# Fused attention and FFN block on one core: moved squares in two halves, the qkv weight split, one LayerNorm and the low parts placed elsewhere

## What is computed

```python
h = _layernorm(x, axis=-1) * (1 + ca) + sa
# _L0_attn_ref: 16 query heads in 4 groups, each group with one key and one value head, D = 128
qkv = jnp.einsum('bsh,ph->bsp', x, weight_qkv).reshape(b, s, NKV, GROUP)
scores = jnp.einsum('bsgqd,btgd->bgqst', q, k) * scale
attn = jax.nn.softmax(jnp.where(causal, scores, jnp.finfo(scores.dtype).min), axis=-1)
out = jnp.einsum('bgqst,btgd->bsgqd', attn, v).reshape(b, s, NH * D)
x = x + ga * jnp.einsum('bse,he->bsh', out, weight_proj)
h = _layernorm(x, axis=-1) * (1 + cb) + sb
x = x + gb * _L0_ffn_ref(h, ...)   # Hadamard transforms, up and gate (1024), silu, down
```

## Time and profile before

| | us |
|---|---|
| median of 3 runs | 1001.2 |
| lowest and highest | 998.78, 1009.32 |
| the profiled execution | 1000.3 |
| its span in the trace | 998.5 |
| turns 0 to 7 in the trace | about 50 to 840 |
| of these turn 3 | about 362 to 464 |
| FFN weights and FFN | about 840 to the end |

### The profile page before, as it was taken

How to read it: one execution, slowest core, us unless ns; L and a number is a source line. 1 busy time by engine, 2 the same in 40 slices (tenths; PEclk the granted TensorE clock), 3 DMA queues, 4 the chain that set the end, 5 groups by cost and what they waited for, 6 DMA issues and landing times.

```text
span 998.5 us, 14544 instructions
## 1 busy us (share of the span) xinstructions
PE 925.7 (93%) x5140; PEld 797.4 (80%) x5140; DVE 641.3 (64%) x1342; ACT 510.5 (51%) x1062; POOL 567.5 (57%) x687
## 2 busy tenths in 40 slices
PE   6979999899889998999899989999999899999998
PEld 5767788878778887888778877787878787888887
DVE  6566658666866576647664767476747666775554
ACT  3456556654556465646564646465646665431111
POOL 1466928792778277837793678458846876120000
PEclk9989999999989998999999989999999999999999
DMA  6033203320322033202420062105210413000000
GB/s 229 1 117 116 74 2 116 117 74 1 116 86 85 22 92 109 86 22 64 137 85 22 32 169 65 43 32 169 64 43 32 117 43 96 1 2 22 21 21 21
DMA packets 31204, 68.99 MB, mean 69 GB/s; under 512 B 3616, under 2 KB 19232, under 8 KB 29984
## 3 DMA queue, kind: packets, MB, share of 16 engines
q1 hardware_dynamic: 30416, 67.91, 21.9%
q10 hardware_dynamic: 720, 0.21, 0.1%
HBM read 42.16 MB, written 25.95 MB: 68 GB/s over the span
## 4 chain that ended last, share of the span: by engine, by line
PE 54%; DMA 16%; POOL 10%; DVE 10%; ACT 5%; issue 2%; SPq 2%; DVEq 0%; POOLq 0%; ACTq 0%
PE ps L1090 14%; PE ps L1091 14%; PE ps L1092 13%; DMA raw_down<-spill 9%; DMA spill<-blocks 6%; PE ps L1216 3%; DVE ps L984 3%; POOL w_lo L631 2%; PE ps L1201 2%; POOL prob L612 2%; PE ps L1207 2%; PE ps L1204 2%; POOL pt_lo L621 2%; SPq L500 2%; ACT prob L721 2%
## 5 line engine op out<-in xcount | busy, mean ns | idle before, releaser
L721 ACT ACTIVATE prob<-ps,nmax 128x1024 f32<-128x1024 f32 (+7 forms) x256 | 189.9, 742 | 129.8 <-DVE nmax L984 128.0
L612 POOL TENSOR_SCALAR prob<-prob,rinv 128x1024 f32<-128x1024 f32 (+7 forms) x256 | 191.8, 749 | 53.1 <-POOL rinv L609 53.1
L984 DVE CUSTOM_DVE_ANT_0 ps<-ps,mask_f 128x1024 f32<-128x1024 f32 (+7 forms) x256 | 191.4, 756 | 39.2 <-PE ps L1207 38.9
L988 DVE TENSOR_TENSOR pt_lo<-ps,pt_hi 128x512 fp32r<-128x512 f32 x197 | 135.5, 688 | 87.1 <-ACT pt_hi L746 85.9
L609 POOL TENSOR_TENSOR rinv<-rsum,mone 128x1 f32<-128x1 f32 x256 | 142.2, 555 | 77.3 <-ACT prob L721 76.2
L621 POOL TENSOR_TENSOR pt_lo<-raw_down,pt_hi 128x512 fp32r<-128x512 f32 x91 | 117.2, 1287 | 119.8 <-ACT pt_hi L751 119.8
L1090 PE MATMUL ps<-pt_hi,v_hi 128*128 128x512 f32 x288 | 132.6, 460 | 32.0 <-DVE pt_lo L988 16.5
L746 ACT ACTIVATE pt_hi<-ps 128x512 fp32r<-128x512 f32 x197 | 117.1, 594 | 74.7 <-PE ps L1216 73.6
L1201 PE MATMUL ps<-k_hi,q_hi 128*128 128x512 f32 (+4 forms) x384 | 115.9, 356 | 21.7 <-ACT prob L721 21.7
L1216 PE MATMUL ps<-ident,prob 128*128 128x128 f32 x788 | 119.5, 276 | 0.8 <-DVE pt_lo L988 0.6
L1091 PE MATMUL ps<-pt_lo,v_hi 128*128 128x512 f32 x288 | 116.2, 403 | 0.0
(11 more groups left out here) (138 smaller groups left out, 1918.2 us busy)
## 6 DMA issues: line engine op xcount, KB each, us to landing
spill<-blocks SPq DMA_DIRECT2D x15, 768.0 KB, 3.3
raw_down<-spill SPq DMA_DIRECT2D x60, 192.0 KB, 4.1
spill<-blocks SPq DMA_DIRECT2D x8, 1024.0 KB, 3.8
raw_down<-spill SPq DMA_DIRECT2D x32, 256.0 KB, 4.8
...
raw_down<-spill SPq DMA_DIRECT2D x28, 128.0 KB, 2.9
```

The lines of the kernel that those rows point to most:

```text
L612: g_.tensor_scalar(row(i, h), row(i, h), rinv[:, at, h:h + 1], 1.0, ALU.mult, ALU.mult).then_inc(prob_done, 1)
L721: a_.activation(row(i, h).rearrange("p (a n) -> p a n", a=nb), score_banks(i, h).rearrange("p (a n) -> p a n", a=nb)[:, :, 0:w], ACT.Exp, ...
L984: v_.tensor_tensor_reduce(scores, scores, late, -1.0, 3.0e38, ALU.add, ALU.min, nmax[:, place(n), h:h + 1]).then_inc(max_done, 1)
L988: v_.tensor_tensor(pt_lo[:, n % 4, :], ring(t, "T", n), pt_hi[:, n % 4, :].bitcast(F32), ALU.subtract).then_inc(ptl_done, 1)
```

## The change

Seven edits:
1. The order of pair 1 becomes `bbbssxxxx`: its units are 9, 10, 11 (block 6), 12 and 13 (block 1), 14 to 17 moved (block 6, j = 3 to 6).
2. The LayerNorm items go from pair 1 to pair 2, at units 0, 2, 3, 4 and 5 of it.
3. W stays only in turn 0 and goes to unit 3 of pair 1. For later weights "WH" (POOL, high part) stands at unit 4 of pair 3, behind S7.0 and T31, and "WL" (DVE, low part in three pieces of 128x512) behind the V of units 5, 6 and 7 of pair 3 (for turns 0 to 5).
4. SP loads the second `w_raw` at the start, later ones behind the group of block 6, and `wp_raw` behind the group of block 5.
5. A group of moved squares travels in halves of two heads: one store behind the second X and one behind the fourth, then four loads for each half (half the bytes each).
6. The low part of every second moved unit is made by DVE instead of POOL: with the new numbering units 7, 14, 16, 23, 26 and 35 on DVE, 6, 8, 15, 17, 25 and 32 on POOL.
7. The columns of a transposed unit are kept in the order block, head, column, so that a half is contiguous; the evictions of O bring them back to head order.

```diff
-ORDER = ("bbbsbbxxx", "bbbsxsxxx", "bbbssxsxx", "bbbssxssx")
+ORDER = ("bbbsbbxxx", "bbbssxxxx", "bbbssxsxx", "bbbssxssx")
-            if p == 1:
-                for k, what in ((0, "LF"), (3, "LN"), (5, "L"), (6, "LH"), (7, "LL")):
+            if p == 2:
+                for k, what in ((0, "LF"), (2, "LN"), (3, "L"), (4, "LH"), (5, "LL")):
                     fill[k].append((t, what, 0, 0))
-            if p == 2 and t + 1 < TURNS:
+            if p == 1 and t == 0:
                 fill[3].append((t, "W", 0, 0))
+            if p == 3 and t + 2 < TURNS:
+                fill[4].append((t + 1, "WH", 0, 0))
+                for k in range(3):
+                    squares[5 + k].append((t + 1, "WL", k, 0))
...
+        def on_pool(n):
+            return MOVED.index(n) % 2 == 0
...
             def swap_blocks(t, i):
-                g, size = GROUPS.index((t, i)), len(group_units(i))
-                sp.wait_ge(block_done, squared(t, i, QPG - 1))
-                sp.dma_start(spill[g % 2, :, 0:size * CH], blocks[:, 0:size * CH]).then_inc(spill_s[g % 2], 16)
-                sp.wait_ge(*spilled(t, i))
+                g, size = GROUPS.index((t, i)), len(group_units(i)) * QB * 2
+                for half in range(2):
+                    sp.wait_ge(block_done, squared(t, i, 2 * half + 1))
+                    sp.dma_start(half_of(spill[g % 2, :, :], i, half),
+                                 half_of(blocks[:, :], i, half)).then_inc(spill_s[g % 2][half], 16)
                 if g:
                     t_of, i_of = GROUPS[g - 1]
-                    sp.wait_ge(el_done, max(entered(t_of, n) for n in MOVED if UNITS[n][0] == i_of))
-                for kb in range(NB):
+                    for n in [n for n in MOVED if UNITS[n][0] == i_of][-2:]:
+                        sp.wait_ge(*low_done(t_of, n))
+                for half in range(2):
+                    sp.wait_ge(*spilled(t, i, half))
+                    for kb in range(NB):
...
+                if what == "WH":
+                    pool.wait_ge(wraw_s, (t + 2) * 16)
+                    pool.wait_ge(qkv_done, this(qkv_done, t, 12))
+                    split_w()
...
+                if what == "WL":
+                    dve.wait_ge(w_hi_s, t + 1)
+                    at = slice(n * 2 * D, (n + 1) * 2 * D)
+                    last = v_.tensor_tensor(w_lo[:, :, at], w_raw[:, :, at], w_hi[:, :, at].bitcast(F32), ALU.subtract)
...
+                if what == "E" and not on_pool(n):
+                    dve.wait_ge(eh_done, entered(t, n))
+                    v_.tensor_tensor(by_head(pt_lo, n), swapped_tile(n), by_head(pt_hi, n).bitcast(F32),
+                                     ALU.subtract).then_inc(el_dve, 1)
...
-                    a_.activation(o_hi[:, out_slot(i), :], O[i], ACT.Copy).then_inc(oh_done, 1)
+                    a_.activation(heads(o_hi[:, out_slot(i), :]), by_heads(O[i]), ACT.Copy).then_inc(oh_done, 1)
...
-                        last = tr(ring(t, "T", n)[:, q * P:(q + 1) * P], row(i, q, j * P, (j + 1) * P), ident[:, :])
+                        last = tr(of_head(ring(t, "T", n), q), row(i, q, j * P, (j + 1) * P), ident[:, :])
```

More of the change, by code:

```diff
@@ L322, in build @@
         t_done, pth_done, ptl_done = sem("transposed"), sem("pt_hi_done"), sem("pt_lo_done")
-        block_done, spill_s, swap_s = sem("blocks_turned"), [sem(f"blocks_spilled{n}") for n in range(2)], [sem(f"blocks_swapped{n}") for n in range(2)]
-        eh_done, el_done = sem("swapped_hi_done"), sem("swapped_lo_done")
+        block_done = sem("blocks_turned")
+        spill_s = [[sem(f"blocks_spilled{n}{half}") for half in range(2)] for n in range(2)]
+        swap_s = [sem(f"blocks_swapped{n}") for n in range(2)]
+        eh_done, el_dve, el_pool = sem("swapped_hi_done"), sem("swapped_lo_by_vector"), sem("swapped_lo_by_pool")
         pv_done, oh_done, ol_done = sem("pv_done"), sem("o_hi_done"), sem("o_lo_done")
@@ L369, in squared, with spilled, low_done, half_of @@
             return SQUARED.index((t, i, h)) + 1
-        def spilled(t, i):
+        def spilled(t, i, half):
             g = GROUPS.index((t, i))
-            return spill_s[g % 2], (g // 2 + 1) * 16
+            return spill_s[g % 2][half], (g // 2 + 1) * 16
         def landed(t, i):
             g = GROUPS.index((t, i))
-            return swap_s[g % 2], (g // 2 + 1) * 16 * NB
+            return swap_s[g % 2], (g // 2 + 1) * 16 * NB * 2
+        def on_pool(n):
+            return MOVED.index(n) % 2 == 0
+        def low_done(t, n):
+            mine = [(u, m) for u, m in ENTERED if on_pool(m) == on_pool(n)]
+            return el_pool if on_pool(n) else el_dve, mine.index((t, n)) + 1
+        def half_of(tile, i, half):
+            size = len(group_units(i)) * 2 * P
+            return tile[:, half * size:(half + 1) * size]
         def swapped_tile(n):
@@ L955, in _ @@
                     gates()
+                if what == "WL":
+                    dve.wait_ge(w_hi_s, t + 1)
+                    at = slice(n * 2 * D, (n + 1) * 2 * D)
+                    last = v_.tensor_tensor(w_lo[:, :, at], w_raw[:, :, at], w_hi[:, :, at].bitcast(F32), ALU.subtract)
+                    if n == 2:
+                        last.then_inc(w_ready, 1)
                 if what == "GB":
                     if n == 0:
-                        dve.wait_ge(*spilled(t, WINDOWS[-1][0]))
+                        for half in range(2):
+                            dve.wait_ge(*spilled(t, WINDOWS[-1][0], half))
                     gate_down(n)
+                if what == "E" and not on_pool(n):
+                    dve.wait_ge(eh_done, entered(t, n))
+                    v_.tensor_tensor(by_head(pt_lo, n), swapped_tile(n), by_head(pt_hi, n).bitcast(F32),
+                                     ALU.subtract).then_inc(el_dve, 1)
                 if what == "X":
                     g, mine = GROUPS.index((t, n)), group_units(n)
-                    if h == 0 and g:
-                        dve.wait_ge(*spilled(*GROUPS[g - 1]))
+                    if h % 2 == 0 and g:
+                        for half in (0, 1) if len(group_units(GROUPS[g - 1][1])) != len(mine) else (h // 2,):
+                            dve.wait_ge(*spilled(*GROUPS[g - 1], half))
                     dve.wait_ge(prob_done, this(prob_done, t, scored(n, h)))
-                    v_.transpose(blocks[:, 0:len(mine) * CH].rearrange("p (k j h q) -> p j k h q", k=NB, j=len(mine), h=QPG)[:, :, :, h, :],
+                    v_.transpose(half_of(blocks[:, :], n, h // 2).rearrange("p (k j h q) -> p j k h q", k=NB, j=len(mine), h=2)[:, :, :, h % 2, :],
                                  row(n, h, mine[0] * P, (n + 1) * P).rearrange("p (j k q) -> p j k q", j=len(mine), k=NB)
```

47 lines of the change are left out of this document (29 added, 18 removed).

## The result

The changed kernel has a median of 1038.8 us (1033.8 to 1042.9, four runs) against 1000.0 us for the kernel before, ratio 1.035, 95% interval 1.031 to 1.040. The profiled execution took 1041.1 us.

A forecast was written before the change was run, and what follows sets the result against it. PE, 93% busy, was taken as the bound, so only its waits and clock could give a gain. Idle time 89, clock 8 and port 5 made 102 against 75.6, 27 us more: 1027 us, 2.6% slower, range 1012 to 1040.

The forecast's parts named there:

- the walk: The new list followed engine by engine through turn 3: 11.35 us of PE waits in each of turns 2 to 5.
- V15 and Y1: Pair 1, block 1's last unit: the chain over DVE and ACT leaves PE 2.25 us of wait.
- L: PE's LayerNorm transposes, now in pair 2: PE waits 1.9 us there for xhat.
- first chunk: Behind L in pair 2: PE waits 2.3 us for the last exponential.
- S0.0, V34 and Y3: End of pair 3: PE waits 1.2, 2.0 and 1.0 us, 3.9 over what it had, in six turns.
- Turn 1: Put at 12.9 us of idle time, with GB at the end of pair 3 as well: 1.5 more.
- the port: DVE low parts with two SBUF inputs blocked beside POOL: 0.6 us a turn on the path, 5 in all.
- the rival's full price: Two thirds of 9.5 us on the path from DVE operations beside POOL, 5.7 a turn more: 1065 us; chance 0.07.
- the clock: PE's lower granted clock behind new waits: 1 us a turn, 8 in all, against 23 before.
- The halves bring nothing: Half-length loads cost as much each, block 6 lands 3 us later, PE waits return: 1039 us; chance 0.08.
- The engines keep up: L, Y1 and the first chunk find their inputs there: 974 us; chance 0.18.
- The end of pair 3 costs nothing: DVE doesn't stand at WL 0, 25 us and 4 of clock go: 998 us, no difference; chance 0.15.

The follow-up runs named there:

- low_pool: Changed kernel with all low parts of moved units on POOL again: 991.1 us.
- low_alt: w_pool3 with every second low part of moved units on DVE: 1000.0 us.
- whwl: w_pool3 with WH at unit 4 of pair 3, three low pieces on DVE, turn 0's W in pair 1, `w_raw` one group earlier: 988.1 us.
- w_pool3: Kernel before with halves, kept column order, later W whole on POOL at unit 3 of pair 3, weight loads behind block 5's group: 960.1 us.
- one_input: Changed kernel with DVE's low parts of moved units replaced by a same-size operation with one SBUF input (low part not computed): 1027.8 us.
- w_only: Kernel before, blocks travelling whole, with only W made whole on POOL at unit 3 of pair 3 and its loads behind the last exchanges: 985.7 us.
- w_back: Changed kernel with the weight whole on POOL at unit 3 of pair 3, turn 0's in pair 2, weight loads behind block 5's group: 1028.2 us.
- wh_early: Changed kernel with WH one unit earlier, in front of the normalisation of S7.0: 1031.6 us.
- order_new: w_pool3 with pair 1 in the change's order: 955.3 us.
- ln_late: w_pool3 with LayerNorm in pair 2 as the change has it: 967.1 us.

## Why the direction was right and the sum 12 us short

**Right: where PE would wait.** Every place of the walk is in the timeline above, with about its size: V5, Y0 and S5.0 together 1.0 (measured 0.23 + 0.39 + 0.37 = 0.99), V15 and Y1 2.25 (0.62 + 2.04 = 2.66), L 1.9 (1.71), first chunk 2.3 (2.17), S0.0, V34 and Y3 3.9 over what was there (0.99 + 1.67 + 0.66 = 3.32). (For V15 and Y1 the prediction's own addends, 8.17 + 0.2 + 0.6, make 9.0 and not 8.8, which brings its 2.25 closer to the 2.66.) Turns of "104 to 106" take 105.5, and DVE's wait in front of WL 0 is 2.17 where 2.3 was said. Turn 0, put at 14.25, has 2.39 + 4.61 + 1.71 + 2.16 + 0.96 + 1.67 + 0.66 = 14.2; there W stands in front of V15, and Y1 doesn't wait, as the step said. Turn 6, put at 8.5, has 8.4. That the chain over DVE and ACT sets the time, and not the load of POOL, is what low_pool (-47.7), low_alt (+39.9) and whwl (+28.0) showed.

**A little too large: the walk.** Turn 1 was put at 12.9 and has 10.3: S0.0 waits 0.2 longer than elsewhere and Y3 not at all, so GB's 1.5 us don't show in the waits. But the clock was at its lower level there for 6.8 us, and Y3 doesn't wait at the end of turn 5 either, under the same level and without GB; the two causes aren't separated. In the middle turns the listed waits are 10.85 with the port's share in them, where 11.35 and 0.6 stood. Over the execution the listed waits grew by 94.7 - 66.1 = 28.6 us. PE's busy time grew by 11.6, of which 1.9 is clock and 9.7 is not; the share of a middle turn in that is the 94.33 less 93.34 of the two stretches above, 1.0 us. It is not the kept column order, since w_pool3 has it too and 93.36 a turn; it comes with the number of waits, 77 listed against 38. In an unbroken stream value products of 0.40 us begin 0.24 us apart, each over the end of the last; the one behind a wait lasts 0.50 with nothing beside it (628.90 above, and 0.40 at 629.23 and at 629.47). A wait so adds up to 0.25 us to PE's busy time, and 39 more of them up to 9.8, the size of the growth; a middle turn has six more, up to 1.5 us for its 1.0. The prediction had no term for it. Together 38.3, where walk and port had 36.4 + 5 = 41.4.

**Too small: the port.** The prediction took 0.6 us a turn on the path, 5 in all. one_input shows 11, about 1.4 a turn: 45 operations were longer by 281 ns (947 - 666), 12.6 us in all, and nearly all of it lay on the path, where the prediction said that "half the rest lies in slack". Its 0.6 doesn't follow from its own words either: half of 9.5, and half of that, is 2.4 a turn. What kept the true number at 1.4 is that a lengthened low part lost 0.4 to 0.7 us as a rule and not 1.06. In pair 1 DVE has no slack, as the walk itself had found at Y1; there the cost should have been taken in full. It was still far from the rival's full price, 5.7 a turn more: 23 of the 45 were not lengthened at all. (That rival's 1065 takes the port's 5 us off twice; its own terms make 1070.) What the walk alone should have said is therefore 38.3 - 11 = 27 and not 36. Its waits by themselves were 19 us too large (28.6 - 11 = 17.6 against 36.4), and the busy time of 9.7 that it left out hid half of that.

**Wrong: the clock.** "I take 1 us a turn, 8, against 23." Measured 24.9 in the profiled execution and 17 to 23 in the others. This is the step that failed, and at 17 us (9 in the mildest of the four) it is the largest of the misses. The prediction argued that of the waits of 1.9 to 2.3 us in the kernel before only some were followed by the low level. In the changed kernel three of them stand close together (Y1, L and the first chunk within 24 us), and in turns 0 to 2 and 6 the lower level followed on one or more. Behind Y1 at 739.10 in turn 6 (2.04 us of wait):

```profile
740.00:743.40 3.40, 3.40 (x17) 3.36 (x16) 0.89 (x3) 0.67 (x2) 1.64 (x3) 0.50 0.66 202
```

And behind Y1 at 631.90 in turn 5, the same wait to a hundredth:

```profile
631.90:635.30 3.40, 3.40 (x25) 3.31 (x26) 2.14 (x6) 1.01 (x3) 2.54 (x4) 1.00 0.43 146
```

17 matmuls in the one, 25 in the other. So the wait right in front doesn't decide alone; no run here separates what does, and that stays open. What the table shows is how the loss goes with idle time and with the size of its pieces. With 44 us of idle time it is 1 to 2 us, with 50 to 51 it is 5 to 9, with 89 to 102 it is 19 to 26. Between 67 and 73 it goes with the pieces: before and w_only, with 38 listed waits each of 1.7 and 1.6 us on average, lose 23.0 and 15.8; low_alt, low_pool and whwl, with 76, 69 and 69 of 0.9 to 1.0, lose 10.0, 6.9 and 8.9. This is one profiled execution for each kernel and a pattern, not a cause.

**The sum again.** Forecast 26.4 over the profiled execution; clock +17, port +6, walk -9: 40.4. The profiled executions stand 1041.1 - 1000.3 = 40.8 apart. That the sum came within 12 us is in part luck: the walk's 9 too much hid as much of the 23 that clock and port had too little.

**The rivals.** "The halves bring nothing" has the right number, 1039, and is false: w_pool3 against w_only shows 25.6 us for them, and ACT's waits of 37.5 us for moved blocks are 2.2 in the changed kernel. "The engines keep up" was to be seen by a wait under 0.5 at L; it is 1.7. "The end of pair 3 costs nothing" had 29 us on it; w_back, without the weight's split, gives 10.6, and wh_early, without the wait in front of S0.0, 7.2.

**Where the change's gain went.** The halves (25.6), the earlier weight (14.3) and the order (4.7) are worth 44.6 us. On w_pool3 LayerNorm's later place costs 7.0, the split of the weight with what came with it in whwl 28.0 and the alternating low parts 39.9, 74.9 together; all at once they cost 8.5 more: 1000.0 - 44.6 + 74.9 + 8.5 = 1038.8. (The 8.5 is what is left over, and with three medians from another set of runs it is uncertain by several us; by the ratios it is 12.5.) That the sum nearly closes hides that the parts cover for one another: taken off the changed kernel the split of the weight gave 10.6 and not 28.0, the alternating low parts 47.7 and not 39.9. And with the new order and the late LayerNorm the low parts cost more than alone: w_back lies 66 us above 962.4, the sum of w_pool3, order_new and ln_late (a kernel that was not run).
